# A second buffer set for the reloaded features of odd chunks, and another order of ACT's and DVE's work

## The reference

```
x = x + L0(groupnorm(x)):
    feats  = four depthwise 7-tap convolutions: row, column, two diagonals
    attn   = softmax over the four of (leaky_relu(mean(feats^2) @ w1) @ w2)
    out    = conv3x3( sum over the four of attn * feats )
x = x + L1(groupnorm(x)):
    q,k,v  = 1x1 convs; q,k softmaxed over the pixels; context = k v^T, out = context q, 1x1 conv
    x_fft  = real FFT path: 1x1, gelu, 1x1, inverse FFT -> qf, normalised; with k: channel attention
    kf, vf = depthwise 3x3 of a 1x1 conv of out
    result = 1x1 conv( channel attention applied to vf )
```

## Time and profile before

| | |
|---|---|
| median of the runs | 3883.88 us |
| the profiled execution's own time | 3878.01 us |
| its span, first to last instruction | 3876.4 us |
| PE busy | 3284.9 us (85%) |
| DVE busy | 2636.5 us (68%) |
| ACT busy | 1536.4 us (40%) |
| POOL busy | 901.2 us (23%) |
| DMA | 455.89 MB, mean 118 GB/s |
| mean granted PE clock | 0.93 |

### The profile page before, as it was taken

The page is one execution under the profiler, slowest core; times in us unless marked ns, Lnnn a source line. Parts: engine busy times, 40 slices in busy tenths (PEclk is TensorE's granted clock), DMA queues, the critical chain, the costliest instruction groups (busy, mean ns, idle before and its releaser), DMA issues.

```text
span 3876.4 us, 55809 instructions
## 1 busy us (share of the span) xinstructions
PE 3284.9 (85%) x19102; PEld 2643.4 (68%) x19102; DVE 2636.5 (68%) x2943; ACT 1536.4 (40%) x2991; POOL 901.2 (23%) x1337
## 2 busy tenths in 40 slices
PE   4567989778998889869898798987899878988998
PEld 2355769657687577757777476875768757776867
DVE  7967777687857778577785777768785777854020
ACT  4412762136511564126631266203652156411540
POOL 1011322205122051211422132220512205121112
PEclk8778999889999899989999899988999889999999
DMA  5494236922478134862359423692237823483013
GB/s 128 109 227 109 71 82 151 237 69 68 93 169 206 50 85 99 210 158 56 79 111 241 105 71 85 146 240 69 70 91 168 206 52 80 104 201 101 1 38 65
DMA packets 222595, 455.89 MB, mean 118 GB/s; under 512 B 137408, under 2 KB 138640, under 8 KB 220240
## 3 DMA queue, kind: packets, MB, share of 16 engines
q1 hardware_dynamic: 169680, 268.83, 29.0%
q0 software_dynamic: 41472, 142.35, 16.2%
q10 hardware_dynamic: 11136, 40.81, 4.5%
HBM read 198.00 MB, written 155.71 MB: 91 GB/s over the span
## 4 chain that ended last, share of the span: by engine, by line
PE 47%; DVE 16%; DMA 15%; issue 9%; POOL 5%; ACT 4%; SPq 2%; ACTq 1%; DVEq 0%; POOLq 0%
DMA feat<-feats_d 10%; PE banks L1143 7%; PE banks L1131 7%; DVE feat L870 6%; PE banks L1113 6%; PE banks L1114 6%; POOL z L496 4%; PE banks L1172 3%; PE banks L1149 3%; PE banks L1195 3%; PE banks L1150 3%; PE banks L1185 3%; DMA feat<-in_x 2%; PE banks L1120 2%; DVE feat L991 2%
## 5 line engine op out<-in xcount | busy, mean ns | idle before, releaser
L870 DVE SCALAR_TENSOR_TENSOR feat<-xin,wt,feat 128x1152 f32<-128x1152 f32 x1116 | 1527.1, 1435 | 324.5 <-ACT feat L614 322.6
L1113 PE MATMUL banks<-e_hi,wp_a 128*96 128x384 f32 x1728 | 623.5, 361 | 175.7 <-DVE x L948 140.1
L1114 PE MATMUL banks<-e_lo,wp_b 128*96 128x384 f32 x1728 | 616.1, 357 | 0.0
L496 POOL COPY z<-vrow 96x192 f32<-96x192 f32 x384 | 397.0, 1070 | 765.9 <-ACT vrow L673 764.6
L1113 PE MATMUL banks<-e_hi,a_a 128*96 128x384 f32 x1656 | 562.9, 340 | 0.0
L1114 PE MATMUL banks<-e_lo,a_b 128*96 128x384 f32 x1656 | 560.8, 339 | 0.0
L1113 PEld LDWEIGHTS banks<-e_hi,wp_a 128*96 128x96 f32 x1728 | 301.5, 174 | 226.5 <-DVE x L948 121.1
L466 POOL DMA_DIRECT2D ring<-e_hi x576 | 293.0, 533 | 651.7 <-PE banks L1120 424.2
L1143 PEld LDWEIGHTS banks<-mats,z 96*96 96x96 f32 x3072 | 303.9, 173 | 95.7 <-issue 53.9
L1143 PE MATMUL banks<-mats,z 96*96 96x96 f32 x3072 | 307.7, 257 | 43.7 <-POOL z L496 40.9
L1114 PEld LDWEIGHTS banks<-e_lo,wp_b 128*96 128x96 f32 x1728 | 301.6, 175 | 30.3
(11 more groups left out here) (168 smaller groups left out, 4681.9 us busy)
## 6 DMA issues: line engine op xcount, KB each, us to landing
feat<-feats_d SPq DMA_DIRECT2D x224, 432.0 KB, 7.5
feats_d<-feat SPq DMA_DIRECT2D x160, 432.0 KB, 4.0
ring<-e_hi POOLq DMA_DIRECT2D x576, 97.2 KB, 4.7
feat<-in_x SPq DMA_DIRECT2D x64, 432.0 KB, 9.3
feats_d<-feat SPq DMA_DIRECT2D x192, 144.0 KB, 2.1
res<-in_x POOLq DMA_DIRECT2D x96, 288.0 KB, 5.7
out<-x POOLq DMA_DIRECT2D x96, 288.0 KB, 3.8
out<-res POOLq DMA_DIRECT2D x96, 288.0 KB, 4.7
```

What stands on the lines that cost most here:

```text
L496: pool.tensor_copy(z[:, :, 2 * g:2 * g + 2], vrow[:, g % VROWS, :, 0:C].rearrange("p r c -> p c r")).then_inc(z_turned, 1)
L870: dve.scalar_tensor_tensor(out=dst, in0=src, scalar=wt[:, q % VARIANTS, d * KT + k:d * KT + k + 1], in1=dst, op0=ALU.mult, op1=ALU.add).th ...
L1113: pe.matmul(dst, wa[:, t, :], rows_l(e_hi, a0, n, dx), start=(t == CENTRE_FIRST[0]), stop=False)
L1114: pe.matmul(dst, wb[:, t, :], rows_l(e_lo, a0, n, dx), start=False, stop=False)
```

## The change

The reloads of odd chunks (1, 3, 5, 7) go elsewhere: directions 0 to 2 into `xin`, direction 3 into `etile`. So a reload of chunk ch waits for chunk ch-2 instead of ch-1, and those of chunk 1 only for the last taps and the last use of `etile`. As the border of `xin` is overwritten, POOL clears it again after the last chunk, and the first two input loads wait for that. Besides: every second turning copy is made by ACT straight from PSUM; LEAD is 9, so one more unit lies before the attention weights; FIRST_UNIT is 3; the logits and the final copies come one tile earlier; the sums beside the next image's first taps have other places.

```diff
-LEAD = 8
+LEAD = 9
+CLEAR_AT = sum(SUMS_AFTER)
-HID_AT = 7
-FIRST_UNIT, UNIT_TIME = 25.0, 17.2
+HID_AT = 6
+FIRST_UNIT, UNIT_TIME = 3.0, 17.2
...
-        per_slot = [nstat[s] + NCH - 1 for s in range(DIRS)]
+        per_slot = [nstat[s] + NCH // 2 - 1 for s in range(DIRS)]
...
-        def slot_free(b, ch, k):
-
-            return (b * NCH + ch - 1) * DIRS + min(k + 2, DIRS)
+        def product_buffer(ch, d):
+
+            if ch % 2 == 0:
+                return feat[0:C, d]
+            if d == DIRS - 1:
+                return etile[:].rearrange("p t n -> p (t n)")
+            return xin[0:C].rearrange("p a r x -> p (a r x)")[:, d * CR * W:(d + 1) * CR * W]
+
+        def buffer_free(b, ch, d):
+
+            k = (d - ch) % DIRS
+            return (b * NCH + ch) * DIRS + (DIRS if k == 0 else k + 1)
...
@@ load_xin
+                if q < 2 and not first_image(b):
+                    sp.wait_ge(xin_cleared, b * 2)
+                    apart(sp)
@@ start (SP)
-                        wait(sp, combo, slot_free(b, 0, n))
+                        wait(sp, combo, 0 if first_image(b) else buffer_free(b - 1, NCH - 2, stat_slot(n)))
@@ step (SP)
+                sp.wait_ge(tap_done, unit_taps(b, UNITS - 1, KT - 1, 0 if first_image(b) else 1))
+                apart(sp)
+                if first_image(b):
+                    sp.wait_ge(last_dir_sums, VARIANTS * PASSES)
+                if second:
+                    sp.wait_ge(e_ready, b * U_E)
+                    apart(sp)
                 for ch in range(1, NCH):
...
-                        wait(sp, combo, slot_free(b, ch, k))
-                        sp.dma_start(feat[0:C, d], feats_d[d, :, ch * CR * W:(ch + 1) * CR * W]).then_inc(feat_loaded[d], 16)
+                        else:
+                            sp.wait_ge(combo, buffer_free(b, ch - 2, d))
+                            apart(sp)
+                        sp.dma_start(product_buffer(ch, d), feats_d[d, :, ch * CR * W:(ch + 1) * CR * W])\
+                            .then_inc((other_loaded if ch % 2 else feat_loaded)[d], 16)
@@ step (POOL)
-                    for g in range(U_KV):
+                    for g in range(0, U_KV, 2):
...
+                            if j == CLEAR_AT:
+                                pool.wait_ge(combo, (b + 1) * NCH * DIRS)
+                                apart(pool)
+                                for x0 in (0, XP - PAD):
+                                    pool.memset(xin[:, :, :, x0:x0 + PAD].rearrange("p a r x -> p (a r) x"), 0.0)\
+                                        .then_inc(xin_cleared, 1)
@@ kv_rows (ACT)
-                    if g >= VROWS:
-                        act.wait_ge(z_turned, i * U_KV + g - VROWS + 1)
+                    if g >= VROWS and g % 2 == 0:
+                        act.wait_ge(z_turned, i * (U_KV // 2) + (g - VROWS) // 2 + 1)
                     act.activation(vrow[:, g % VROWS, :, 0:C], ps[:, :, 0:C], ACT.Exp)
+                    if g % 2:
+                        act.activation(z[:, :, 2 * g:2 * g + 2], ps[:, :, 0:C].rearrange("p r c -> p c r"), ACT.Exp)
@@ step (ACT)
-                    copies(min(NG, HID_AT + ch), min(NG, HID_AT + 1 + ch) if ch < NCH - 1 else NG)
+                    copies(min(NG, HID_AT + ch + (ch >= 4)), min(NG, HID_AT + 1 + ch + (ch >= 3)) if ch < NCH - 1 else NG)
@@ start (DVE)
-                taps(b, 0, hooks=[(2, between), (6, between), (10, between)])
-                taps(b, 1, 0, EARLY_TAPS, hooks=[(2, between), (6, between)])
+                taps(b, 0, hooks=[(2, between), (5, between), (8, between), (11, between)])
+                taps(b, 1, 0, EARLY_TAPS, hooks=[(2, between)])
@@ step (PE)
-                    attention_block(b - 1, {(HID_AT, 0): hidden, (HID_AT, 1): logits} if first else {})
+                    attention_block(b - 1, {(HID_AT - 1, 1): hidden, (HID_AT, 0): logits} if first else {})
```

More of the change, by code:

```diff
@@ L279, in build @@
         z_turned = sem("z_turned")
+        other_loaded = [sem(f"other_loaded{i}") for i in range(DIRS)]
+        xin_cleared = sem("xin_cleared")
         waits_passed = {e.engine: sem(n) for e, n in (
@@ L338, in summed @@
             return (ch + k) % DIRS
-        def slot_free(b, ch, k):
-            return (b * NCH + ch - 1) * DIRS + min(k + 2, DIRS)
+        def product_buffer(ch, d):
[7 more added lines that the diff above has]
+            return (b * NCH + ch) * DIRS + (DIRS if k == 0 else k + 1)
         def combo_loaded(b, ch, d):
-            return feat_loaded[d], (b * per_slot[d] + nstat[d] + ch) * 16
+            if ch % 2:
+                return other_loaded[d], (b * (NCH // 2) + ch // 2 + 1) * 16
+            return feat_loaded[d], (b * per_slot[d] + nstat[d] + ch // 2) * 16
         def res_loads(b, j):
@@ L974, in products @@
                 flat = acc[:].rearrange("p r c -> p (r c)")
-                part = feat[0:C, summed(ch, 0)]
+                part = product_buffer(ch, summed(ch, 0))
                 for k in range(k0, k1):
@@ L990, in products @@
                                 dve.wait_ge(pads_zero, PADS)
-                        ins = dve.scalar_tensor_tensor(out=flat if k == DIRS - 1 else part, in0=feat[0:C, d],
+                        ins = dve.scalar_tensor_tensor(out=flat if k == DIRS - 1 else part, in0=product_buffer(ch, d),
                                                        scalar=l0v[:, 8 + d:9 + d], in1=part, op0=ALU.mult, op1=ALU.add)
@@ L1140, in dft @@
                             if at == AT_DFT2:
-                                pe.wait_ge(z_turned, (i + 1) * U_KV)
+                                pe.wait_ge(z_turned, (i + 1) * (U_KV // 2))
                         for c in range(4):
```

## The result

The changed kernel takes 3709.63 us in the median of four runs (3705.26 to 3715.08), the kernel before 3883.59 us (3882.89 to 3897.43) on the same chip: 0.9545 of the time, 95% interval 0.952 to 0.957. That is 174 us less; 182 were forecast. The profiled execution took 3710.5 us with a span of 3709.0, 167.4 us less than the span before.

The account below looks back on a forecast made before the run. Bound by late feature reloads with full DMA engines, and by POOL's turning copies in the attention stage. Saving 7 x 17 + 7 + 7 x 8 = 182 us gave 3700 us, range 3640 to 3795.

Parts of the forecast that it names:

- The sum: Whole kernel: 7 x 17 + 7 + 7 x 8 = 182 us saved, giving about 3700 us.
- step 3: Attention stage: half of POOL's turning copies to ACT, stage 51 instead of 59.6 us; 8 us in seven images, bounds 0 and 13.
- Step 1, second buffer set: Convolution stage: earlier residual load and faster chunks, 17 us per image at the fifth sum, 7 for image 0; bounds 4 and 21.
- Rival A: DMA stays the bound, head start lost to other traffic: 4 us per image from the second buffers, 3796 us; chance 0.16.
- Step 4, the earlier logits and copies: Convolution stage: earlier attention logits, hidden after tile 5, worth nothing, with 25 us of room.
- Step 4, the tap order: Attention stage: earlier ACT pieces and one more unit before the weights; cost 0, gain 0, bounds -2 to +5 per image.
- Step 2: Before the next input loads: two POOL memsets clear the pads; cost 0, at most one sum, 2 us.
- The sum hooks: Next image's first taps: four sums in the first 11 taps of unit 0 instead of over 14; cost 0.
- The signs listed: Trace signs: earlier reloads, near-zero reload waits, DMA share under 1 before first sum, turning stage 51 us, period about 435.
- B: Convolution and turning-copy gains both at their upper ends: 233 us saved, time 3651 us; chance 0.12.
- C: Tap units keep their slow pace, 22.7 us at the slowest, delaying the exponential tiles: 3919 us; chance 0.05.
- D: Gains of one stage are eaten by the next, residual or input loads as late as now: within 0.5%; chance 0.05.

Follow-up runs that it names:

- buffers alone: Kernel before with only the second buffer set, its waits and the clearing of the pads: 3784.49 us, ratio 0.9742.
- order alone: Changed kernel without the second buffer set, keeping ACT's half of the turning copies, new tap order, logits and hooks: 3779.56 us, ratio 0.9733.
- late copies: Changed kernel with logits and final copies of the e convolution as late as before (HID_AT 7): 3751.83 us, ratio 0.9659.
- late taps: Changed kernel with logits and final copies as late as before and the old tap order (LEAD 8, FIRST_UNIT 25): 3683.67 us, ratio 0.9484.
- all on POOL: Changed kernel with all 48 turning copies on POOL again: 3754.82 us, ratio 0.9663.
- early residual loads: Changed kernel with the residual loads of the first two row groups issued ahead of the others: 3692.07 us, ratio 0.9505.
- the two with the added wait: Changed kernel with DVE waiting once per image for POOL's first turning copy: 3644.72 us; the same plus early residual loads: 3627.42 us.

## Why the prediction was right, and which steps were not

**The sum.** It was 15 + 6 x 25 + 17 = 182 against the profiled execution, which gave 13.3 + 6 x 22.6 + 18.3 = 167. The missing 15 us are nearly all in the period, 2.4 in each, and 2.1 of these in one place, the stage of step 3.

**Step 1, second buffer set: the size is shown, the cause only by half.** 17 us were forecast at the fifth sum, and 142.9 + 44.9 became 134.2 + 36.3, which is 17.2 before rounding. The second half, the chunk pace, is the buffers' own: 8.7 us with the buffers alone, none without them. The first half is not: order alone gives 9.4, buffers alone 3.7. The text said the last final copy was late and the residual load would keep its 6.9 us. The copy was as forecast. But with the second buffer set the load keeps that time only when the products start early, so that the reloads of chunks 4 and 5 leave some 10 us sooner; with one set, before and with the order alone, it lands in 4.7 to 8.1 us in every image. Rival A and the page named with it (the Trainium skill, "DMA: Bandwidth & Descriptors", section "Issuing engines are not separate DMA queues": transfers of all issuing engines interleave on the same engines) had this mechanism; this case agrees, though the one seen delayed is the residual load, and the DMA share doesn't tell it: the load takes 7.1 us behind shares of 1.04 and 1.02 in the changed kernel, 12.2 and 11.8 behind 1.05 and 1.04 with the products late.

**Step 4, the earlier logits and copies: failed.** "The earlier attention logits ... are worth nothing" rested on 25 us of room. There was room for the sum's order but not for the DMAs that the products release. Put back, they cost 6.0 us at the first sum, 5.4 a period and 42 in all. A step that is moved moves its transfers, and these were not followed.

**Step 4, the tap order: failed, on the other side.** It was priced at 0. It did what was forecast for DVE: the wait before the weights is 14.2 us (10 or more was said), and the wait for first taps fell from 322.6 to 139.4 us. But by closing DVE's gaps it holds POOL's first copy for 12.1 us. The same edit costs 68 us with late copies (3751.8 against 3683.7). Mended with one wait, the changed kernel gains 65. Without this loss the forecast of 3700 would have been too high by 55.

**Step 3, ACT's half of the turning copies: 5.9 of 8 us a period** (first exp to weights 111.7 to 105.8). The term itself was too small: the stage could give 15 (96.6 with the wait added), more than the upper bound of 13, because PE keeps its pace of about 0.96 us a step (46.2 us) beside tap work too; without the new tap order ACT's half gave 14.3 a period (buffers alone against late taps). The long copy takes 9.2 of it. Taking ACT's half away costs 6.1 a period, with the long copy in both kernels.

**Step 2**, clearing the pads: cost 0 as forecast. It runs at 1588.44, the first input load leaves at 1598.28. The sum hooks cost nothing either: from the fifth sum to the second group norm it takes 70.5 us with the old ones (buffers alone) and with the new.

**The signs listed.** Chunk 1's reload is issued 17 us before the first product (some 20 were said); waits for reloads in chunks 4 to 7 are 2.2 us or less in all images (after the first sum of the period shown, 0.35); the residual load is still waited for and the first sum comes 8.7 us earlier; the period is 438 (435); the last input load leaves 18 us earlier against the weights (1609.20 against 1685.16). Two did not hold: the DMA share before the first sum is 1.04 and 1.02, not under 1; and the turning stage takes 56.3 us (1748.9 to 1805.2), not 51. The second one was the sign of the failed step.

**Rivals.** A would have needed no gain in pace; B's 3651 is near what this kernel gives once the gap is made (3644.7). C, slow tap units, did not come: 48 taps ran at 1.33 us each. Nor did D: 167 us of the gains reached the end.

The right number is thus partly luck: a gain of 15 us a period in one stage was taken for 8, and a loss of 9 in the same stage for none.

## What to carry to other kernels

When an edit closes the idle gaps of DVE, look at the longest and not only the mean instruction of POOL beside it: one copy of 12 us hides in a median of 1.0, and a wait that makes a single gap can be worth more than the work it delays. When a step is moved earlier or later, follow the transfers that its end releases up to the small load on the critical path that they will share the DMA engines with. Two halves of a change that gain 98 and 103 us alone can have one place in common; measure them together before adding.

## What the runs showed of the hardware

**POOL held by DVE.** In five kernels (changed, order alone, all on POOL, late copies, early residual loads) the first turning copy fell into an unbroken run of DVE's multiply-adds with two SBUF inputs, in 35 images: each time it took 11.8 to 12.1 us and ended 0.24 us behind the last multiply-add of the run. In the five others that have POOL copies (before, buffers alone, late taps, the two with the added wait), also 35 images, it fell into a gap and took 0.38 us, and the later ones took turns with DVE, 1.6 us at most. The Trainium skill ("SBUF — State Buffer", section "SBUF: two separate sides") gives an exclusive lock for a whole instruction to whichever starts first; the turns agree with that (a copy 1.5 us beside taps and 0.38 alone), a wait over nine taps isn't told there. Why only the first copy after 87 to 90 us of POOL's idleness is held, while a later one gets in within one tap, stays open, as does whether a much longer run would hold it longer: in all 35 images the run ended 11.6 to 11.9 us after the copy began. In the five of these in which it ended 0.3 us sooner, the copy ended 0.3 us sooner too.

**A small load behind large ones.** The residual load of 288 KB lands 4.7 to 8.1 us after its issue where none to two reloads of 432 KB had not landed yet when it was issued, and in 11.3 to 13.2 us where five or six had (three kernels: buffers alone, late copies, late taps). In the three with early residual loads it is three to five, and 7.9 to 11.7 us. How long before the load the last reload left doesn't tell it: in the period shown, 15 us in the changed kernel and 6 in the kernel before, with 7.0 and 6.9 us to landing. In the kernel before, one or two are under way, since each reload waits for its one buffer. The GB/s of those stretches are 258 in the changed kernel and 266 and 280 with five under way. That the unlanded reloads are what delays it isn't shown by a run of its own: none moved the reloads alone.
